# An expert layer whose stationary operand changes sides: weights staged by ScalarE, the hidden layer born transposed

## What is computed

```python
x = x + xattn(layernorm(x), ctx_2048, w_qkv, w_proj, b_proj)      # 16 heads, 8 batches of 256 tokens
x = x + ffn(layernorm(x), conf_w, conf_b, gate_w, up_w, down_w, wealth)

def ffn(x, ...):                                    # E = 8 experts, 2 of them for each token
    bids = sigmoid(x @ conf_w.T + conf_b) * wealth
    top_bids, selected = top_k(bids, 2)
    combine = sum(one_hot(selected, 8) * softmax(top_bids))
    g, u = x @ gate_w[e].T, x @ up_w[e].T           # 128 -> 512
    expert_out[e] = (silu(g) * u) @ down_w[e].T     # 512 -> 128
    return einsum("ebsh,bse->bsh", expert_out, combine)
```

## Time and profile before

| | |
|---|---|
| time, median of 3 runs | 541.78 us (535.16 to 543.32) |
| the profiled execution: time, span | 540.74 us, 539.1 us |
| PE busy, share of the span | 484.7 us, 90% |
| DVE | 356.6 us, 66% |
| ACT | 289.8 us, 54% |
| POOL | 181.4 us, 34% |
| mean granted TensorE clock | 0.961 of full |
| slot loop, first gate matmul to the landing of the last store | 382.57 to 521.09 us |

### The profile page before, as it was taken

The page is one execution under the profiler, slowest core; times in us unless marked ns, Lnnn a source line. Parts: engine busy times, 40 slices in busy tenths (PEclk is TensorE's granted clock), DMA queues, the critical chain, the costliest instruction groups (busy, mean ns, idle before and its releaser), DMA issues. The chain is left out here.

```text
span 539.1 us, 10943 instructions
## 1 busy us (share of the span) xinstructions
PE 484.7 (90%) x3635; PEld 302.4 (56%) x3636; DVE 356.6 (66%) x646; ACT 289.8 (54%) x584; POOL 181.4 (34%) x381
## 2 busy tenths in 40 slices
PE   2489999999999999999999987988899999999930
PEld 1255555555555555555555544987566666666620
DVE  7798798797888887987889822589143333333316
ACT  1237777777787777777787875310133333333310
POOL 6141231412312412313200001004467666666620
PEclk9999999999999999999999998786999999999985
DMA  6512234333243343332222000800111111111126
GB/s 180 124 43 58 72 84 108 79 107 100 74 125 85 93 121 85 90 81 55 53 63 55 24 2 2 234 1 1 24 36 41 39 39 39 39 43 40 35 83 171
DMA packets 32255, 38.12 MB, mean 71 GB/s; under 512 B 5604, under 2 KB 20580, under 8 KB 32212
## 3 DMA queue, kind: packets, MB, share of 16 engines
q1 hardware_dynamic: 27252, 30.79, 21.1%
q0 software_dynamic: 2560, 5.25, 3.8%
q10 hardware_dynamic: 2400, 1.51, 1.0%
HBM read 16.58 MB, written 4.72 MB: 40 GB/s over the span
## 5 line engine op out<-in xcount | busy, mean ns | idle before, releaser
L463 DVE TENSOR_REDUCE max_part<-max_ps 128x2 f32<-128x1024 f32 (+1 forms) x192 | 226.0, 1221 | 39.1 <-PE max_ps L561 30.8
L422 ACT ACTIVATE probs<-ring_ps 128x512 f32<-128x512 f32 x384 | 198.4, 604 | 50.9 <-PE ring_ps L584 47.7
L584 PE MATMUL ring_ps<-blocks,keys 64*128 64x512 f32 x384 | 151.7, 473 | 2.0 <-ACT probs L422 1.5
L594 PE MATMUL pv_ps<-probs,value_cols 128*32 128x256 f32 x1536 | 103.4, 388 | 0.0
L561 PE MATMUL max_ps<-keys,blocks 64*128 64x512 f32 x256 | 84.3, 448 | 7.5 <-DMA blocks<-masked 6.4
L584 PEld LDWEIGHTS ring_ps<-blocks,keys 64*128 64x128 f32 x384 | 65.6, 187 | 31.5 <-ACT probs L422 25.2
L1018 DVE TENSOR_TENSOR hidden<-up_ps,silu 128x512 f32<-128x512 f32 x40 | 27.7, 692 | 80.9 <-PE up_ps L1116 78.7
L911 ACT ACTIVATE hiddenT<-at_ps 128x512 f32<-128x512 f32 x40 | 23.9, 597 | 75.6 <-PE at_ps L1133 67.0
L338 POOL CAST maxes<-rowmax 128x8 fp32r<-128x8 f32 x32 | 6.3, 197 | 171.2 <-DVE rowmax L470 171.2
L594 PEld LDWEIGHTS pv_ps<-probs,value_cols 128*32 128x32 f32 x1536 | 40.3, 109 | 40.2 <-issue 15.1
L561 PEld LDWEIGHTS max_ps<-keys,blocks 64*128 64x128 f32 x256 | 42.3, 196 | 26.7 <-issue 16.6
(11 more groups left out here) (150 smaller groups left out, 492.1 us busy)
## 6 DMA issues: line engine op xcount, KB each, us to landing
keys<-parts SPq DMA_DIRECT2D x96, 96.0 KB
blocks<-masked SPq DMA_DIRECT2D x93, 64.0 KB
ctx_v_sb<-ctx_v_dram SPq DMA_DIRECT2D x8, 256.0 KB, 2.9
gate<-gateT_dram SPq DMA_DIRECT2D x8, 256.0 KB, 2.8
up<-upT_dram SPq DMA_DIRECT2D x8, 256.0 KB, 2.9
y_in<-pick_outs SPq DMA_DIRECT2D x8, 256.0 KB, 5.1
raw<-ctx_kT_dram SPq DMA_DIRECT2D x7, 256.0 KB, 2.7
h_rows<-h SPq DMA_DIRECT2D x4, 256.0 KB, 5.0
```

What stands on the lines that cost most here:

```text
L422: act.activation(probs[par][:, k, PAIR * a:PAIR * (a + 1)], bank("exp", s * XUNITS + u)[:].rearrange("p (g n) -> p g n", n=N), ACT.Exp).th ...
L463: vec.reduce_max(out, bank, axis=AX.X).then_inc(max_done, 1)
L584: pe.matmul(ps[:], keys[rows, t, k * P:(k + 1) * P], blocks[rows, t], start=True, stop=True)\
L594: mm = pe.matmul(pv_ps[ROWS * g:ROWS * (g + 1), 0:N], value_cols[:, t, k, g, :], probs[q % 2][:, k, g, :], start=(k == 0), stop=(k == KT - 1))
```

## The change

The first layer of the experts changes its operands' sides. Before, `xT` was stationary and the weights moved, so that the output had tokens in its rows; now four pieces of 128 columns of the weights are stationary in turn and `xT` moves (`hidden_rows`), so that the output of each piece has hidden units in its rows and tokens in its columns: it is already the `hiddenT` that the second layer wants. The four transposes, their bank `at_ps`, their copy by ACT and the tile `hidden` go, and DVE's product is written straight into `hiddenT`. The weights of a slot's expert are no longer read in place through a register: ACT copies them, 128 x 512 of gate and 128 x 512 of up, into one of two buffers `staged`, one slot ahead (`stage`), and reads the expert's number for it. The second layer and the copy of its output stand one slot later than their slot instead of two, and DVE does `copy_xT` ahead of the product. `slots` runs one step less. POOL's program is unchanged.

```diff
             act.wait_ge(gap_ready, 2)
             act.activation(weight[:], gap[:], ACT.Sigmoid).then_inc(weights_done, 1)
 
+            def stage(j, r):
+                e = act.value_load(table[0:1, bass.ds(j, 1)], min_val=0, max_val=E - 1)
+                wait_for(act, up_filled, j - 1)
+                act.activation(staged[:, r % 2, 0], m.gate[:, bass.ds(e, 1), :].rearrange("p a i -> p (a i)"), ACT.Copy)\
+                   .then_inc(gate_staged, 1)
+                act.activation(staged[:, r % 2, 1], m.up[:, bass.ds(e, 1), :].rearrange("p a i -> p (a i)"), ACT.Copy)\
+                   .then_inc(up_staged, 1)
+
             def step(i, r):
                 j = 4 * i + r
+                if exists(i, r, 1):
+                    stage(j + 1, r + 1)
                 if exists(i, r, 0):
                     act.wait_ge(gate_filled, j + 1)
                     wait_for(act, act_done, j - 1)
                     act.activation(silu[:, r % 2, :], gate_ps[r % 2][:], ACT.Silu).then_inc(silu_done, 1)
-                if exists(i, r, -1):
-                    act.wait_ge(actT_filled, j)
-                    wait_for(act, y_filled, j - 2)
-                    act.activation(hiddenT[:, (r - 1) % 2], at_ps[(r - 1) % 2][:].rearrange("p (c n) -> p c n", n=P),
-                                   ACT.Copy).then_inc(actT_copied, 1)
-
-            slots(act, step, SLOTS_PAD + 1)
+
+            act.wait_ge(table_ready, 1)
+            act.wait_ge(m.gate_up_in, 32 * E)
+            stage(0, 0)
+            slots(act, step, SLOTS_PAD)
             n = TILES // CHUNKS
             for c in range(CHUNKS):
                 act.wait_ge(summed, 2 * n * (c + 1))
...
 
             def step(i, r):
                 j = 4 * i + r
+                if exists(i, r, 1):
+                    copy_xT(j + 1, r + 1)
                 if exists(i, r, 0):
                     vec.wait_ge(silu_done, j + 1)
                     vec.wait_ge(up_filled, j + 1)
-                    wait_for(vec, actT_filled, j - 1)
-                    vec.tensor_tensor(hidden[:, r % 2, :], up_ps[r % 2][:], silu[:, r % 2, :], ALU.mult)\
+                    wait_for(vec, y_filled, j - 1)
+                    vec.tensor_tensor(hiddenT[:, r % 2].rearrange("p c n -> p (c n)"), up_ps[r % 2][:], silu[:, r % 2, :], ALU.mult)\
                        .then_inc(act_done, 1)
-                if exists(i, r, 1):
-                    copy_xT(j + 1, r + 1)
-                if exists(i, r, -2):
-                    vec.wait_ge(y_filled, j - 1)
-                    if not isinstance(i, int) or j >= 6:
-                        vec.wait_ge(y_stored[(r - 2) % 4], (i if r >= 2 else i - 1) * 16)
-                    vec.tensor_copy(y_out[:, (r - 2) % 4, :], y_ps[:, 0:C]).then_inc(y_copied, 1)
+                if exists(i, r, -1):
+                    vec.wait_ge(y_filled, j)
+                    if not isinstance(i, int) or j >= 5:
+                        vec.wait_ge(y_stored[(r - 1) % 4], (i if r >= 1 else i - 1) * 16)
+                    vec.tensor_copy(y_out[:, (r - 1) % 4, :], y_ps[:, 0:C]).then_inc(y_copied, 1)
 
             copy_xT(0, 0)
-            slots(vec, step, SLOTS_PAD + 2)
+            slots(vec, step, SLOTS_PAD + 1)
             for t in range(TILES):
                 if t % (TILES // CHUNKS) == 0:
                     vec.wait_ge(y_loaded[t // (TILES // CHUNKS)], 32)
...
 
             def idle(turns):
                 for _ in range(turns):
-                    pe.matmul(at_ps[0][:, 0:P], m.ident[:], m.ident[:], start=True, stop=True)
+                    pe.matmul(spare_ps[:, 0:P], m.ident[:], m.ident[:], start=True, stop=True)
 
             idle(20)
             pe.wait_ge(router_in, 48)
...
                 wait_for(pe, xT_copied, j)
                 pe.transpose(xT_ps[:, 0:P], x_in[:, r4, :], m.ident[:]).then_inc(xT_filled, 1)
 
+            def hidden_rows(ps, weights, x):
+                for c in range(IC):
+                    mm = pe.matmul(ps[:, c * P:(c + 1) * P], weights[:, c * P:(c + 1) * P], x, start=True, stop=True)
+                return mm
+
             def step(i, r):
                 j = 4 * i + r
                 if exists(i, r, 0):
-                    e = expert(j)
                     pe.wait_ge(xT_copied, j + 1)
+                    pe.wait_ge(gate_staged, j + 1)
                     wait_for(pe, silu_done, j - 1)
-                    pe.matmul(gate_ps[r % 2][:], xT[:, r % 2, :], m.gate[:, bass.ds(e, 1), :].rearrange("p a i -> p (a i)"),
-                              start=True, stop=True).then_inc(gate_filled, 1)
+                    hidden_rows(gate_ps[r % 2], staged[:, r % 2, 0], xT[:, r % 2, :]).then_inc(gate_filled, 1)
+                    pe.wait_ge(up_staged, j + 1)
                     wait_for(pe, act_done, j - 1)
-                    pe.matmul(up_ps[r % 2][:], xT[:, r % 2, :], m.up[:, bass.ds(e, 1), :].rearrange("p a i -> p (a i)"),
-                              start=True, stop=True).then_inc(up_filled, 1)
+                    hidden_rows(up_ps[r % 2], staged[:, r % 2, 1], xT[:, r % 2, :]).then_inc(up_filled, 1)
                 if exists(i, r, 1):
                     transpose_x(i, r, 1)
-                if exists(i, r, -2):
-                    e = expert(j - 2)
-                    pe.wait_ge(actT_copied, j - 1)
-                    wait_for(pe, y_copied, j - 2)
+                if exists(i, r, -1):
+                    e = expert(j - 1)
+                    pe.wait_ge(act_done, j)
+                    wait_for(pe, y_copied, j - 1)
                     for c in range(IC):
-                        mm = pe.matmul(y_ps[:, 0:C], hiddenT[:, r % 2, c, :],
+                        mm = pe.matmul(y_ps[:, 0:C], hiddenT[:, (r - 1) % 2, c, :],
                                        down[:, bass.ds(e, 1), c, :].rearrange("p a h -> p (a h)"),
                                        start=(c == 0), stop=(c == IC - 1))
                     mm.then_inc(y_filled, 1)
-                if exists(i, r, -1):
-                    pe.wait_ge(act_done, j)
-                    wait_for(pe, actT_copied, j - 2)
-                    for c in range(IC):
-                        mm = pe.transpose(at_ps[(r - 1) % 2][:, c * P:(c + 1) * P],
-                                          hidden[:, (r - 1) % 2, c * P:(c + 1) * P], m.ident[:])
-                    mm.then_inc(actT_filled, 1)
 
```

8 lines of the change are left out of this document (4 added, 4 removed).

## The result

The changed kernel takes **551.78 us** (median of 4 runs, 551.21 to 554.02) against 540.97 us before on the same chip (535.16 to 543.32): a ratio of 1.0244, interval 1.0156 to 1.0333. So it is slower; that it is slower by more than 2% is not shown. Times here are medians over all runs of a kernel, while ratios and intervals leave out runs in a second, slower state of the chip (four of the ten of `e11_short_rows`, at 552 to 554 us, and one of `e12_pool_waits_landing`). The forecast was 519.4 us, with a range of 515 to 529.

A forecast was written before the change was run, and what follows sets the result against it. PE was taken to bound the slot loop at 3.16 us a slot, falling to 2.81. Last gate 387.9 + 37 x 2.81 = 491.9, plus a 6.8 us tail, gave 498.7 instead of 521.09: 22.4 saved, 519.4 us, range 515 to 529.

The forecast's parts named there:

- First layer: Gate and up on PE: each becomes eight 128-column passes, 0.89 instead of 0.86 us, adding 0.06 us a slot.
- transposes away: Four transpose passes, 0.44 us a slot, are removed from PE.
- PE's slot 2.78 to 2.81: PE's slot falls from 3.16 us to 2.78, taken as 2.81 with 0.03 allowed for pass boundaries.
- ScalarE's copies: ACT's two staging copies a slot, 0.60 us each (bounds 0.4 to 0.9), within an ACT chain of 2.6 us.
- Cost: nothing, hidden by 2.81 us of PE work: ACT's staging one slot ahead: may begin 1.94 us after a gate began, is wanted 3.7 us later, so adds no time.
- DVE's order: DVE copies tokens (0.28 us) ahead of the product (0.69), ending at gate + 2.37, before the next gate at gate + 2.78.
- Head: Loop start: slot 1's gate at 385.1 instead of 385.69, slot 2's at 387.9, POOL's step-2 load at about 389.6.
- Tail: Loop end: from the last gate to the last landing, 6.8 us.
- Lag of the second layer: Output copied one step earlier, so POOL sends ahead: gap before its load 0.15 to 0.2 us, step about 2.88.
- Rival 1: POOL is the bound: gap stays 0.47, step 3.1 to 3.17 us, 528 us (525.5 to 529.5); chance 27%.
- Rivals 2 and 3: ACT or handshake sets 2.95 to 3.25 us slots, 525 to 536 (10%); or staging copies cost 1.2 us each, 556 (3%).
- rival 4: Short matmuls run slower: sixteen added weight loads stand alone, 632 us, or the clock falls, roughly doubling the loop; chance 2%.

The follow-up runs named there:

- e11_short_rows: Changed kernel with POOL's indirect DMAs kept in number and order but moving 64 bytes of each row instead of 512; 543.46 us, ratio 1.0043.
- e12_pool_waits_landing: Changed kernel in which POOL's step also waits until the load of its step before has landed; 546.65 us, ratio 1.0116.
- e9: Changed kernel with rows moved by plain DMAs that SP issues instead of POOL's indirect ones, gather and scatter left out; 518.1 us, ratio 0.9552.
- e4: Changed kernel with ScalarE staging weights for slots 0 and 1 only, later slots reusing them; 537.85 us, ratio 0.9955.
- e3: Changed kernel with the second layer two slots behind again and hiddenT in four buffers instead of two; 550.95 us, ratio 1.0225.
- e17: Changed kernel with SP's plain DMAs, plus 76 unused indirect loads on POOL, each behind the landing of the load six before; 612.1 us, ratio 1.137.
- e16: Changed kernel with staging, input transpose and its copy two slots ahead, second layer two behind, more buffers, POOL's store later; 543.29 us, ratio 1.0069.
- e5: Kernel before the change with POOL's store one slot later, so that POOL can work ahead; 542.26 us, ratio 1.0034.

## Why the prediction was wrong, point by point

- *First layer, 0.89 us each; transposes away; PE's slot 2.78 to 2.81.* Right: 2.79 us in e9, and in the kernel after wherever POOL isn't at two DMAs in a row (2.89 from gate to gate with a restart in it).
- *ScalarE's copies 0.60 each, hidden.* 0.631 and 0.61 us: right in size, and hidden as long as `up` is seen in time (e9). But the step "Cost: nothing, hidden by 2.81 us of PE work" counted no slack for a late `up`: without the copies (e4) 14 of the 34 us lost come back.
- *DVE's order.* Right; its copy ends in time in e9.
- *Head.* Gates at 385.08 and 387.97 and the load at 389.37, forecast 385.1, 387.9 and 389.6.
- *Tail.* Last gate at 527.28, last landing 532.61 + 2.25 = 534.86: 7.6 us for 6.8. The last output's matmuls stood at the copy of the one before (0.73 us).
- *Lag of the second layer.* **Here it failed.** The prediction says that "POOL's sequencer can send ahead", that the gap ahead of the load shrinks to 0.15 to 0.2 us and that "POOL would then be at about 2.88, a hair slower than PE". It happened: the gap is 0.15 and the step 2.75 us (447.81 to 450.56 in the rows above), even a little under PE's 2.78. That the new lag brings it about is not so: in e3, with the old lag, results are late in the same way. But what failed is the price: the sum took a full POOL to cost only what POOL's own step costs. It held POOL's 60% beside PE's full busy time in the earlier trace rows to be independent, and priced no effect of the one on the other. The runs showed that POOL's indirect DMAs in close order hold TensorE's completions by up to 2.7 us in this kernel, and that the next gate waits for them. Measured: 551.8 - 518.1 = 33.7 us from the loop without POOL's DMAs to the kernel after, of which the clock's four falls in the loop (3.41 us each at 0.50, 16 passes of 0.22 instead of 0.11 in each) are at most 7.
- *Rivals.* Rival 1 had the right engine and the wrong price: with POOL as the bound it gave 528, and no complete version with the new first layer came below 543. Rivals 2 and 3 named ACT, whose work measured 0.61 to 0.63; rival 4's two halves both missed, though the clock did fall four times, in a loop in which PE now waits; in e9, where it doesn't wait, the granted clock stayed at 1.00 through the loop until 499 us. Rival 4's sum also counted sixteen added weight loads; four of them stood in the old first layer already, so twelve were added.
- *The sign was there.* In the trace of before, ACT's copy of the transposes started up to 0.6 us after their recorded end (445.02 for matmuls that end at 444.44 in the rows above). It cost nothing there, so I didn't ask why.

## What to carry to other kernels

Read a full engine's wait against the recorded end of what it waits for, not against the wait's name: where a copy starts a microsecond behind the matmul that releases it, or the profile says "remote", something outside the two is at work. GpSimd's indirect DMAs in close order are felt by TensorE's readers: before making the rest of a loop faster, work out what share of a step this issuing would take where GpSimd doesn't wait. No run here gives a safe share; 26%, one load in 3.6 us, was clean; at 48% the loop lost 2.6 us of 111, at 62% (the kernel before) one result came up to 0.6 us late in about half of the slots, and at 72% the gain was lost and more. And a change that removes a wait lets an engine run fuller; price what that does to the others, not only what it does to the engine.

## What the runs showed that I had not expected

TensorE's results can be held from their readers by 43 us while GpSimd issues indirect DMAs 0.30 us apart (e17), and for 12 us after it has stopped. In the two kernels with 48 and 60% of issuing the delay is up to 1.0 us, in one with 26% none is seen, and in stretches of 72% it reaches 2.7 us (4.9 in e16). 700 copies on GpSimd do nothing of the kind, and with an eighth of the bytes three quarters of the loss remain. Where it could be told apart (e5, e16, e17) the matmuls behind the late result had gone on, so it is the completion that is held, not the multiplication. What it is inside the chip that the two share is open: no run here shows it. Whether the number of matmul instructions in a slot sets the size of the loss is open too, and whether evenly spaced DMAs would let the kernel before go below 3.28 us a slot.
